# Sixteen-head attentions: row maxima handled by halves of a unit, the second scores 17 steps behind the first

## The reference, cut to what matters

```python
qkv = jnp.einsum('btc,cd->btd', x, w_qkv) + b_qkv                       # L1, causal, 16 heads of 8
scores = jnp.einsum('bhqd,bhkd->bhqk', q, k) * scale
scores = jnp.where(causal, scores, jnp.finfo(scores.dtype).min)
attn = jax.nn.softmax(scores, axis=-1)
out = jnp.einsum('bhqk,bhkd->bhqd', attn, v)
return jnp.einsum('btc,cd->btd', out, w_out) + b_out
...
scores = jnp.einsum('mbhtk,mbhsk->mbhts', q, kk) / jnp.sqrt(jnp.float32(KD))   # L3, M=2 experts, no mask
attn = jax.nn.softmax(scores, axis=-1)
ctx = jnp.einsum('mbhts,mbhsk->mbthk', attn, v)
mha_out = jnp.einsum('mbthk,mhkd->mbtd', ctx, mha_wo) + mha_bo[:, None, None, :]
x = x + jnp.einsum('mbtd,bm->btd', mha_out, mha_probs)
```

## Time and profile before

| | us |
|---|---|
| median of 3 runs | 1903.27 |
| lowest and highest | 1901.16, 1909.96 |
| the profiled execution, its own time | 1909.27 |
| its span in the trace | 1907.6 |
| PE busy | 1636.6 |
| DVE busy | 1277.6 |
| ACT busy | 1157.4 |
| POOL busy | 579.9 |

### The profile page before, as it was taken

One profiled execution on the slowest core, in us unless ns is written; L12 is line 12 of the kernel. 1 busy time (PEld: TensorE's weight loads), 2 busy tenths in 40 slices (PEclk: granted clock), 3 DMA queues, 4 the chain that ended last, 5 costly groups with the idle time before them and its releaser, 6 DMA issues.

```text
span 1907.6 us, 40495 instructions
## 1 busy us (share of the span) xinstructions
PE 1636.6 (86%) x15456; PEld 871.8 (46%) x15456; DVE 1277.6 (67%) x2593; ACT 1157.4 (61%) x2725; POOL 579.9 (30%) x729
## 2 busy tenths in 40 slices
PE   6999899988898989897787948979999596999986
PEld 2555355633556355633343323324555262455535
DVE  5875687546875587537583768357888455788846
ACT  4667466734666466655376565447888554588872
POOL 3651365102652265201463014033322002332200
PEclk9999999999999999999598979978999899799997
DMA  5000000000000000000640000045442101544401
GB/s 195 19 19 7 7 19 19 7 0 6 19 19 8 6 19 18 8 1 18 114 81 2 1 1 0 1 75 101 90 104 57 45 1 35 107 97 102 86 12 57
DMA packets 55022, 75.40 MB, mean 40 GB/s; under 512 B 5744, under 2 KB 38736, under 8 KB 54320
## 3 DMA queue, kind: packets, MB, share of 16 engines
q1 hardware_dynamic: 54832, 72.82, 17.3%
HBM read 46.55 MB, written 16.88 MB: 33 GB/s over the span
## 4 chain that ended last, share of the span: by engine, by line
PE 60%; ACT 14%; DVE 11%; issue 6%; POOL 5%; DMA 3%; SPq 0%; DVEq 0%; POOLq 0%; ACTq 0%
PE ps L197 56%; ACT arena L709 6%; DVE arena L801 2%; ACT arena L1594 2%; DVE arena L845 2%; PE ps L588 1%; ACT arena L270 1%; ACT arena L272 1%; PE ps L1490 1%; DMA arena<-scratch 1%; POOL arena L945 1%; POOL arena L944 1%; DVE arena L933 1%; ACT arena L265 1%; PE ps L1504 1%
## 5 line engine op out<-in xcount | busy, mean ns | idle before, releaser
L197 PE MATMUL ps<-arena 32*64 32x128 f32 (+7 forms) x11176 | 696.4, 304 | 78.7 <-ACT arena L1594 25.8
L197 PEld LDWEIGHTS ps<-arena 32*64 32x64 f32 (+5 forms) x11176 | 404.4, 119 | 364.9 <-issue 113.1
L1594 ACT ACTIVATE arena<-ps 128x512 f32<-128x512 f32 (+1 forms) x640 | 333.9, 576 | 80.6 <-PE ps L197 71.8
L1632 DVE TENSOR_REDUCE arena<-ps 128x2 f32<-128x512 f32 x512 | 322.9, 686 | 76.4 <-PE ps L197 74.3
L197 PE MATMUL ps<-arena,w_L0f 128*128 128x512 f32 (+3 forms) x800 | 325.5, 540 | 31.1 <-DVEq L2623 9.3
L709 ACT ACTIVATE arena<-ps,arena 128x128 f32<-128x128 f32 x512 | 226.7, 460 | 68.3 <-DVE arena L847 67.7
L197 PE MATMUL ps<-arena,const 128*128 128x512 f32 (+1 forms) x536 | 177.6, 616 | 69.3 <-DVE arena L2106 22.1
L197 PEld LDWEIGHTS ps<-arena,w_L0f 128*128 128x128 f32 (+2 forms) x800 | 139.5, 188 | 151.8 <-issue 97.2
L952 POOL TENSOR_TENSOR arena<-arena 128x512 f32<-128x512 f32 x128 | 132.4, 1041 | 155.0 <-DVE arena L831 154.8
L801 DVE TENSOR_TENSOR arena<-ps,arena 128x1024 f32<-128x1024 f32 x128 | 152.1, 1207 | 15.5 <-ACT arena L723 9.9
L723 ACT ACTIVATE arena<-ps 128x512 f32<-128x512 f32 x128 | 76.8, 600 | 102.2 <-DVE arena L801 77.8
(11 more groups left out here) (228 smaller groups left out, 2093.6 us busy)
## 6 DMA issues: line engine op xcount, KB each, us to landing
scratch<-arena SPq DMA_DIRECT2D x40, 384.0 KB, 2.8
arena<-scratch SPq DMA_DIRECT2D x80, 192.0 KB
arena<-scratch SPq DMA_DIRECT2D x80, 128.0 KB
arena<-arena SPq DMA_DIRECT2D x64, 128.0 KB, 2.3
arena<-scratch SPq DMA_DIRECT2D x80, 88.0 KB
arena<-in_experts SPq DMA_DIRECT2D x16, 256.0 KB, 4.2
w_L0f<-in_L0f SPq DMA_DIRECT2D x2, 1557.0 KB, 12.7
arena<-arena SPq DMA_DIRECT2D x80, 12.0 KB
```

The costliest lines, as they stand in the source:

```text
L197: return self.nc.tensor.matmul(o, lhsT, rhs, start=start, stop=stop, skip_group_check=True)
L1594: S.activation(self.pt[g % 4][:, e, 0:both], ps[:, self.shifted_bank(2 * g + e), 0:both], ACT.Exp, scale=self.scale).then_inc(self.exped.s ...
L1632: o = V.tensor_reduce(mx, ps[:, self.score_bank(s), :].rearrange("p (t s) -> p t s", t=2), AXX, ALU.max)
```

## The change

The maxima of a unit are split, turned, copied and written in two halves of eight heads. The lag of the second scores falls from 25 steps to 17. The contexts are made two units behind instead of three. The output projection moves from `i == 11` to `i == 13`, since the first half's turn now stands at `i == 11`; the second half's stays at `i == 3` of the next unit. SP's list gets two more DMAs for each unit, behind the six loads.

```diff
-    PAIRS, QUADS, LAG = HEADS // 2, HEADS // 4, 25
+    PAIRS, QUADS, LAG = HEADS // 2, HEADS // 4, 17
-    NORM_CENTERS, NORM_SQUARES, NORM_MEANS, NORM_INVERTS, NORM_FINISHES = (4, 6, 12), (25, 29, 30), (29, 38, 41), (31, 42, 44), (40, 44, 45)
+    NORM_CENTERS, NORM_SQUARES, NORM_MEANS, NORM_INVERTS, NORM_FINISHES = (4, 6, 12), (17, 19, 20), (19, 22, 24), (21, 24, 27), (22, 26, 28)
...
-        for s in range(-2 * HEADS, HEADS * (self.units + 2) + 14):
+        for s in range(-2 * HEADS, HEADS * (self.units + 1) + 15):
...
+    def half_at(self, s):
+        y, at = divmod(s - 3, HEADS // 2)
+        return y - 1 if at == 0 and 0 <= y - 1 < 2 * self.units else None
...
# TensorE
-            u = k - 1
-            if i == 3 and self.is_unit(u):
-                self.wait_ge(eng, self.mx_split, u + 1)
+            y = self.half_at(s)
+            if y is not None:
+                u = y // 2
+                self.wait_ge(eng, self.mx_split, y + 1)
...
-                    o = mm(ps[0:PARTS * HEADS, 7, t * P:(t + 1) * P], self.mx_parts[u % 2][:, 2 * t:2 * t + 2].rearrange("p e a g -> p (e a g)"), k_.ident_b[:])
+                    o = mm(ps[0:PARTS * HEADS // 2, 7, t * P:(t + 1) * P], self.mx_parts[y % 2][:, 2 * t:2 * t + 2].rearrange("p e a g -> p (e a g)"), k_.ident_b[:])
-            u = k - 3
+            u = k - 2
             if i == 5 and self.is_unit(u):
...
-            if i == 11 and self.ends_batch(u):
+            if i == 13 and self.ends_batch(u):
...
-                if x == 0:
+                if x % (self.PAIRS // 2) == 0:
                     stacked = self.mx_stacked[u % self.STACKS]
-                    eng.wait_ge(stacked.sem, stacked.at(32 * (u // self.STACKS + 1)))
+                    eng.wait_ge(stacked.sem, stacked.at(64 * (u // self.STACKS) + (32 if x == 0 else 64)))
...
# ScalarE
+            y = self.half_at(s)
+            if y is not None:
+                self.wait_ge(eng, self.mx_turned, y + 1)
...
+                S.activation(self.mx_rows[y % 2], ps[0:PARTS * HEADS // 2, 7, 0:SEQ], ACT.Copy).then_inc(self.mx_copied.sem, 1)
...
# GpSimd: the same four operations on half as many columns, at i == 0 and i == 8
-            u = k - 1
-            if i == 0 and self.is_unit(u):
+            y = s // (HEADS // 2) - 1
+            if i % (HEADS // 2) == 0 and 0 <= y < 2 * U:
...
# SyncE
         for k in range(-2, U + 1):
-            u = k - 1
-            if self.is_unit(u):
...
+            if self.is_unit(k - 1):
+                self.store_maxima(eng, 2 * k - 1)
             u = k + 2
...
                         eng.dma_start(to[row:row + n], pair[0:n]).then_inc(stacked.sem, 16)
+            if self.is_unit(k):
+                self.store_maxima(eng, 2 * k)
+
+    def store_maxima(self, eng, y):
+        u, half = y // 2, self.PAIRS // 2
+        st, stacked = self.q[u % self.STACKS], self.mx_stacked[u % self.STACKS]
+        self.wait_ge(eng, self.mx_copied, y + 1)
+        for e in range(2):
+            row, at = 64 * e + self.ROWS, e * PARTS * half
+            eng.dma_start(st[row:row + PARTS, y % 2 * half:(y % 2 + 1) * half, :], self.mx_rows[y % 2][at:at + PARTS * half, :]).then_inc(stacked.sem, 16)
```

More of the change, by code:

```diff
@@ L1371, in __init__ @@
         self.mx = [a.take(2 * HEADS).rearrange("p (t h) -> p t h", t=2) for _ in range(2)]
-        self.mx_rest = a.take(2 * HEADS).rearrange("p (x g) -> p x g", x=4)
-        self.mx_parts = [a.take_bf16(2 * PARTS * HEADS).rearrange("p (x a g) -> p x a g", x=4, a=PARTS) for _ in range(2)]
-        self.mx_rows = [a.take_bf16(SEQ, PARTS * HEADS) for _ in range(2)]
+        self.mx_rest = a.take(HEADS).rearrange("p (x g) -> p x g", x=4)
+        self.mx_parts = [a.take_bf16(PARTS * HEADS).rearrange("p (x a g) -> p x a g", x=4, a=PARTS) for _ in range(2)]
+        self.mx_rows = [a.take_bf16(SEQ, PARTS * HEADS // 2) for _ in range(2)]
         self.pt = [a.take(2 * BANK).rearrange("p (h c) -> p h c", h=2) for _ in range(4)]
@@ L1396, in __init__ @@
         self.stacked = [self.sig(f"stacked{i}", 16 * self.loads * n) for i, n in enumerate(turns)]
-        self.mx_stacked = [self.sig(f"mx_stacked{i}", 32 * n) for i, n in enumerate(turns)]
+        self.mx_stacked = [self.sig(f"mx_stacked{i}", 64 * n) for i, n in enumerate(turns)]
     def steps(self):
-        for s in range(-2 * HEADS, HEADS * (self.units + 2) + 14):
+        for s in range(-2 * HEADS, HEADS * (self.units + 1) + 15):
             yield s, s // HEADS, s % HEADS
@@ L1467, in heads_tensor @@
                 self.wait_ge(eng, self.v_copied, k)
[L1468 to L1469 removed]
+                self.wait_ge(eng, self.ctx_copied, k - 2)
+                self.wait_out(eng, k - 3)
+                self.wait_ge(eng, self.mx_copied, 2 * k - 1)
                 if u == 2:
@@ L1569, in heads_scalar @@
                 self.bias(eng, u)
-            u = k - 1
[L1571 to L1576, removed]
+            y = self.half_at(s)
+            if y is not None:
+                self.wait_ge(eng, self.mx_turned, y + 1)
+                if y >= 2:
+                    v = y // 2 - 1
+                    stacked = self.mx_stacked[v % self.STACKS]
+                    eng.wait_ge(stacked.sem, stacked.at(64 * (v // self.STACKS) + 32 * (y % 2 + 1)))
+                S.activation(self.mx_rows[y % 2], ps[0:PARTS * HEADS // 2, 7, 0:SEQ], ACT.Copy).then_inc(self.mx_copied.sem, 1)
             if i == 7 and self.is_unit(k):
@@ L1655, in heads_gpsimd @@
                 G.affine_select(pt, pt, [[0, 2], [0, 2], [1, P]], ALU.is_ge, 0.0, base=0, channel_multiplier=-1).then_inc(self.selected.sem, 1)
-            u = k - 1
-            if i == 0 and self.is_unit(u):
[L1658 to L1661, removed]
+            y = s // (HEADS // 2) - 1
+            if i % (HEADS // 2) == 0 and 0 <= y < 2 * U:
+                u, z = y // 2, y % 2
+                self.wait_ge(eng, self.topped, HEADS // 2 * (y + 1))
+                self.wait_ge(eng, self.mx_turned, y - 1)
+                mx, parts = self.mx[u % 2].rearrange("p t (e g) -> p (t e) g", e=2)[:, :, self.PAIRS // 2 * z:self.PAIRS // 2 * (z + 1)], self.mx_parts[z]
                 ch.did(G.tensor_copy(parts[:, :, 0, :], mx))
```

28 lines of the change are left out of this document (12 added, 16 removed).

## The result

| | before | after |
|---|---|---|
| median of 4 runs, us | 1905.39 | 2013.28 |
| lowest and highest | 1901.16, 1909.96 | 2001.68, 2021.01 |
| ratio of after to before | | 1.0561, 95% interval 1.0499 to 1.0623 |
| the profiled execution, its own time | 1909.27 | 2017.49 |
| its span | 1907.6 | 2015.7 |

The kernel became 5.6% slower: +108 us where +74 was forecast.

What follows compares the result with a forecast made beforehand. PE was taken to bound the kernel at 13.2 us a unit; a 15.6 us loop through SP's queue would replace it. 1909.27 + 63.2 + 10.7 = 1983.2, or 1977 against the median, range 1925 to 2015.

Steps and rivals of the forecast that it cites:

- The small work: Per unit: second turn at most 0.29 us on PE, second copy 0.38 on ACT; near zero if PE bounds.
- the main forecast: Whole kernel: first half lands late behind SP's loads and closes a loop; 1977 us, own range 1940 to 2010, chance 0.64.
- the range for all: Whole kernel, all cases: 1925 to 2015 us, leaving out at most 2 in 10.
- the loop of 15.6 us: SP's list, units with loads ahead: second half's issues, parts' store, loads to landing, PE to copy; 15.6 us against 13.2.
- the 1.0 that I took for turns and steps: Each stage: last two units' turns +0.6 us and eight steps +0.4 us.
- The eight steps: First to last pair of a stage: 8 more steps hold a first score, 0.83 us against 0.78; +0.4 us a stage.
- Rival B: Stall also costs PE clock, half clock for part of each unit: loop 16.6 to 17.6 us, total 2006 to 2037; chance 0.13.
- the 9.0: SP's queue: first half lands 9.0 us after the loads' first issue; bounds 8.1 and 9.5.
- the three equal landings: Stage starts before the change: maxima landed 9.53, 9.50 and 9.51 us after the loads' first issue, whenever themselves issued.
- A: Halves land in time, 2.4 to 2.6 us after issue; starts gain 4.6 us a stage; 1891, range 1880 to 1903; chance 0.10.
- C: Loop through SP's list not closed, only the wait behind the loads stays: stall 1.5 us a unit, 1949 us; chance 0.10.
- D: Whole kernel: small parts cancel and the landing is only just late; within 0.5%; chance 0.03.

Runs made afterwards that it cites:

- run 1: Changed kernel with the first half's two DMAs moved in SP's list to just ahead of the six loads: 1907.7 us, ratio 1.0015 to the kernel before.
- run 3: Changed kernel's halves and SP order, but lag 25, contexts three units behind, norm steps as before except third centering at 14: 1908.09 us, ratio 1.0036.
- run 5: Changed kernel with only three of the six loads from a stage's fifth unit on, leaving out part of the computation: 1922.94 us, ratio 1.0091.
- run 7: Changed kernel with first half's DMAs ahead of loads in unmasked stages; causal stage with lag 25, contexts three behind, early norm steps: 1896.26 us, ratio 0.9955.
- Run 4: Changed kernel with the first half's two DMAs issued by GpSimd on its own queue instead of by SP: 2011.62 us, ratio 1.0566.
- run 2: Changed kernel with the next parts' store ahead of the second half's DMAs in SP's list, first half still behind the loads: 1993.59 us, ratio 1.0467.

## Why the prediction came out as it did

**Right.** The sign, the place and the mechanism. The chain holds a DMA `arena<-arena` once a unit, PE waits for it at the pair behind the projection, and the loop through SP's list is closed in the order in which it was written down. Runs 1, 3, 5 and 7 each take one member of it away (the place in the list, the early pair, the backlog) and the period is 13.2 to 13.5 again. The last interval of each `L3Attend`, with no loads ahead, is 12.8 (about 13.2 forecast). The small work was rightly costed near nothing (run 3).

The time itself is luck in part. 2013.28 lies 3 us above the 1940 to 2010 that I gave the main forecast, and only 2 us inside the range for all, 1925 to 2015; single executions went from 2001.68 to 2021.01.

**The term that was mis-sized: the loop of 15.6 us.** Its links, as means over the 13 intervals, from the rows of the pair, the copy, the store and the first load:

| us | forecast | first, second `L3Attend` | with two matmuls in the wait |
|---|---|---|---|
| pair to the end of the copy at `i == 3` | 2.3 | 2.94, 3.07 | 2.53, 2.46 |
| two issues, until the store | 1.5 | 1.60, 1.61 | 1.57, 1.57 |
| store to landing | 2.77 | 3.03, 2.97 | 2.96, 2.94 |
| loads' first issue to the next pair | 9.0 | 8.90, 8.92 | 8.97, 8.77 |
| period | 15.6 | 16.48, 16.57 | 16.02, 15.74 |

The link on which the forecast spent most of its argument, 9.0, came out at 8.9 in the mean, 7.5 to 10.0 in single units. The first link is off by 0.7. At full clock it is 2.52 (1351.93 to 1354.46), so the raw copy in between costs 0.2 more than I took. The other 0.4 to 0.6 of the mean is the clock: in a slow unit the link is 3.6 (1398.97 to 1402.55), at a granted 0.55. The store is within 0.05 of its 2.77 in 14 of the 26 units, and 2.87 to 3.98 in the others. The unit at 1398.97 holds both, and its period is 18.0. The chain of waits:

```profile
1398.97 2.69 PE ps L197 x22
...
1402.18 0.37 ACT arena L1586
...
1404.10 3.96 DMA scratch<-arena
1408.08 0.31 SPq L1725
```

Thirteen intervals at 0.9 to 1.0 over the forecast make 24 of the 34 us by which the sum was short. Most of the rest stands in the last two units, which I had taken as nearly unchanged: +4.0 in the first `L3Attend`, where the interval behind the last stall is 16.3 (1519.4 to 1535.7, granted 0.71, PE busy for 15.3 of it), and +5.6 in the causal stage. In run 1, with no stall and at full clock, the unmasked stages' last units take 36.6 and 36.2 us where the kernel before takes 36.2, so there the 1.0 that I took for turns and steps was more than enough; the excess goes with the clock (0.88 granted in the first stage's last units, 1.00 in run 1). The causal stage is different: in run 1 its +3.7 stays (1001.9 to 1043.2 against 998.3 to 1036.0), so this belongs to the lag. In that stretch stand 31 first scores instead of 23, and their matmuls keep PE busy for 13.2 us instead of 10.4 (15.7 in the changed kernel); PE's turns also wait 6.4 us for GpSimd's split instead of 3.1 (4.3). The eight steps that now hold a first score as well cost some 3 us there, where I took 0.4.

**Rival B was partly right.** The stall does cost clock: the loops are granted 0.87 and 0.89 where before they had 0.98. But B priced it at 1 to 2 us in every unit. Only in 17 of the 26 units does the lower level show in the 3 us behind the pair (two of them are the stages' first units, where it shows in the kernel before as well), and holding the clock up with two matmuls gives back 0.46 and 0.83 us. The time landed in B's range (2006 to 2037) by adding a clock loss of half B's size to a loop that was itself a few tenths too short. I gave B as a whole 0.13, because at 95% busy PE had held its clock; that row spoke of steady work, not of work with a hole of 2 us in the mean, up to 3.8, in each 16.5.

**What failed is the reason I gave for the 9.0.** I read the three equal landings as the order within one queue and let the Trainium skill stand behind it (DMA: Bandwidth & Descriptors, section Queues, rings and completion order: descriptors of one ring are consumed in order). Run 4 puts the maxima into a ring of their own and they land no earlier. So the rule may hold, but it is not what set these landings. The row told "by the loads' clock", and that was right; the step from there to the queue was a guess that the three rows could not tell from a backlog shared by all queues. The same section says that a completion write comes after every earlier write of that DMA engine, across its queues. Run 4 doesn't contradict that rule (8.7 us from the loads' first issue, on a queue that held nothing else), but it isn't needed for the delay there, since the maxima's own last data packets start as late as the last of the loads'. The sum did not suffer, since both readings give 9.0, but a cure taken from the wrong one (another queue) would have failed.

**Rivals A, C and D.** A was the right account of a kernel in which the order is mended, for the unmasked stages: the start gains 6.7 and 5.8 us (4.6 forecast). It left out that GpSimd would then bound the causal stage. C is nearest to run 2. Its price of 1.5 us a unit became 2.2 and 2.7 (periods of 15.4 and 15.9 against 13.2). Part of that is the loads that still wait for the copy in 10 of the 26 units, and the clock falls there too (0.94 granted in the first loop); how much each takes is not shown.

## What to carry to other kernels

Where one engine issues both bulk loads and small urgent writes, look at its written list for a closed loop: an issue that waits for work that waits for a transfer behind this same list's loads. Put the small write ahead of the loads; on this chip moving it to another queue bought nothing, while a change of their order bought 105 us. When a stall is removed, look for the engine that used it as cover (here GpSimd in the causal stage), and give each stage its own lag.

## What the runs showed of the hardware that was not expected

- A DMA of 6 KB, issued by GpSimd on a queue that was otherwise empty, needed 5.98 us from its issue to its landing while 816 KB of loads were under way on SP's queue, and its last packet went with theirs; with no loads under way such halves landed 2.3 to 3.2 us after their first issue; in the kernel before, two such writes of 12 KB each were over 2.4 us after their first issue into idle DMA engines.
- A wait of 1.9 us in the mean (none to 3.8) once in 16.5 us lowered PE's granted clock from 0.98 to 0.87 in the mean of a loop, in some units and not in others with the same work. Two matmuls of no use in that wait brought it back to 0.97 and more. Why one unit falls and the next doesn't is left open.
- The store of the parts to HBM took 2.76 to 2.81 us in 14 of the 26 units of the changed kernel's two loops and 2.87 to 3.98 in twelve, with no other DMA issue of this kernel next to it but the second half's. In eleven of the twelve a packet of 8 or 16 KB, on one of the two queues that the page calls `instruction`, starts 0.3 to 1.0 us after the store's issue; of the other 14 units this holds for one. No run isolates it, so this is what two things do together in one trace, and not a shown cause.
